# A ternary feed-forward layer whose down projection takes its activation as two halves in the short format

## The reference

```
def _tlin(x, w, s):
    return jnp.einsum('bsi,oi->bso', x, w) * s
h = jax.nn.silu(_tlin(x, w1_w, w1_s)) * _tlin(x, w2_w, w2_s)
h = jax.nn.gelu(_tlin(h, h1_w, h1_s), approximate=False)
h = jax.nn.gelu(_tlin(h, h2_w, h2_s), approximate=False)
return _tlin(h, w3_w, w3_s)
```

## Time and profile before

| | |
|---|---|
| median of 3 runs | 1860.53 us (1858.65 to 1861.09) |
| profiled execution, its own time | 1849.88 us |
| its span, first to last instruction | 1848.1 us |
| PE busy in the span | 1516.0 us (82%) |
| DVE busy | 1064.0 us (58%) |
| ACT busy | 729.2 us (39%) |
| mean granted clock of TensorE | 0.915 |

### The profile page before, as it was taken

How to read it: one execution, slowest core, us unless ns; L and a number is a source line. 1 busy time by engine, 2 the same in 40 slices (tenths; PEclk the granted TensorE clock), 3 DMA queues, 4 the chain that set the end, 5 groups by cost and what they waited for, 6 DMA issues and landing times.

```text
span 1848.1 us, 26160 instructions
## 1 busy us (share of the span) xinstructions
PE 1516.0 (82%) x8925; PEld 1098.1 (59%) x8925; DVE 1064.0 (58%) x2296; ACT 729.2 (39%) x1214; POOL 103.1 (6%) x129
## 2 busy tenths in 40 slices
PE   7999999777778967777788999999888888873455
PEld 5666666555534435556567787878484848463344
DVE  3434434877777648777883525261667777754222
ACT  2312221666635655445512222222274747561111
POOL 0000000000000000000000000000000000003111
PEclk9999999899989978889899999999989989985777
DMA  9330000300000000000094000001000000001553
GB/s 320 115 114 0 0 0 6 148 11 11 11 1 1 1 11 1 11 11 11 0 340 131 1 2 1 2 1 31 6 2 6 0 5 5 0 0 56 174 156 103
DMA packets 66241, 83.35 MB, mean 45 GB/s; under 512 B 13395, under 2 KB 61004, under 8 KB 65998
## 3 DMA queue, kind: packets, MB, share of 16 engines
q1 hardware_dynamic: 63774, 66.83, 11.9%
q10 hardware_dynamic: 512, 11.11, 1.8%
q0 software_dynamic: 1872, 4.27, 0.6%
HBM read 60.49 MB, written 33.10 MB: 51 GB/s over the span
## 4 chain that ended last, share of the span: by engine, by line
issue 40%; PE 34%; DVE 11%; DVEq 4%; ACT 4%; SPq 2%; DMA 2%; ACTq 1%; POOL 1%; POOLq 0%
PE bank L1756 6%; PE bank L1757 6%; DVE plo L820 3%; PE bank L1819 3%; PE bank L1576 3%; PE bank L1596 2%; PE bank L1578 2%; DMA jx<-copy_routed 2%; PE bank L1530 2%; PE bank L1688 1%; ACT hq L1323 1%; ACT phi L1264 1%; PE bank L1860 1%; ACTq L1322 1%; PE bank L1713 1%
## 5 line engine op out<-in xcount | busy, mean ns | idle before, releaser
L820 DVE TENSOR_TENSOR plo<-e,phi 120x512 f16<-120x512 f32 x256 | 185.5, 740 | 86.8 <-ACT phi L1264 81.0
L1596 PE MATMUL bank<-Q,Kpad 128*120 128x256 f16 x1024 | 209.9, 288 | 8.6 <-ACT MBT L1256 8.6
L1270 ACT ACTIVATE e<-bank 120x512 f32<-120x512 f32 x256 | 152.8, 597 | 68.3 <-PE bank L1601 38.7
L775 DVE TENSOR_REDUCE MB<-bank 128x4 bf16<-128x480 f32 x256 | 149.5, 647 | 17.6 <-PE bank L1578 12.1
L1264 ACT ACTIVATE phi<-e 120x512 f16<-120x512 f32 x256 | 158.1, 622 | 0.0
L1576 PE MATMUL bank<-Kpad,Q 128*128 128x480 f16 x256 | 107.7, 421 | 55.8 <-issue 32.0
L1600 PE MATMUL bank<-MBT,selm 128*120 128x256 bf16 x512 | 144.3, 282 | 0.0
L1601 PE MATMUL bank<-MBT,sels 128*120 128x256 bf16 x512 | 144.0, 281 | 0.0
L1619 PE MATMUL bank<-V,phi 120*128 120x34 f16 (+1 forms) x1024 | 85.4, 176 | 56.0 <-DVE plo L820 54.4
L1596 PEld LDWEIGHTS bank<-Q,Kpad 128*120 128x120 f16 x1024 | 117.3, 138 | 10.7 <-ACT MBT L1256 10.7
L1494 PE MATMUL bank<-xT,winT 128*127 128x512 f32 (+1 forms) x256 | 114.8, 594 | 4.7 <-ACTq L1183 4.7
(11 more groups left out here) (271 smaller groups left out, 2945.2 us busy)
## 6 DMA issues: line engine op xcount, KB each, us to landing
copy_routed<-zeros SPq DMA_DIRECT2D x1, 17028.0 KB, 65.6
jw<-in_w1e SPq DMA_DIRECT2D x23, 256.0 KB, 2.8
jw<-in_w2e SPq DMA_DIRECT2D x23, 256.0 KB, 3.0
h1w<-copy_h1T SPq DMA_DIRECT2D x1, 4096.0 KB, 17.8
h2w<-copy_h2T SPq DMA_DIRECT2D x1, 4096.0 KB, 14.2
ctxp<-in_ctxT SPq DMA_DIRECT2D x13, 240.0 KB, 2.6
jx<-copy_routed SPq DMA_DIRECT2D x23, 132.0 KB, 2.7
jb<-in_b2e SPq DMA_DIRECT2D x23, 128.0 KB, 3.4
```

What stands on the lines that cost most here:

```text
L775: dve.tensor_reduce(MB[:, t, h0 // 8, SK + h0 % 8:SK + h0 % 8 + 4], bank[2 + n % 4][:, 0:4 * SK].rearrange("p (h k) -> p h k", h=4), AX.X, ...
L820: dve.tensor_tensor(plo[:, u % 3, :], e32[:, u % 3, :], phi[:, u % 3, :], ALU.subtract).then_inc(s.lo, 1)
L1270: act.activation(e32[:, u % 3, :], bank[2 + u % 4][0:SK, :], ACT.Exp).then_inc(s.exp, 1)
L1596: pe.matmul(ps, Kpad[:, v, r, g, b * SK:b * SK + SK], Q2[:, g, qs], start=(v == 0), stop=False)
```

## The change

The down projection moves into `second`, and so into both of its copies. It takes the activation as the halves `hah` and `hal`, two passes for each tile of f3, in the short format in the first copy. ScalarE writes the second gelu into `raw` (semaphore `Ff.g2`), and VectorE splits it (`Ff.h2`), after the splits of the next pair's input. VectorE's check in the first pair takes in f3 too. f3 is now copied and loaded as the other matrices are.

```
-        for t, w in ((wq2, "wq2"), (wk2, "wk2"), (wv2, "wv2"), (wo2, "wo2"), (f3, "f3T")):
+        for t, w in ((wq2, "wq2"), (wk2, "wk2"), (wv2, "wv2"), (wo2, "wo2")):
...
+    w_in["f3T"] = nc.dram_tensor("copy_f3T", [HID, D], F32, kind="Internal").ap()
...
+                sp.dma_start(f3[:], kp(w_in["f3T"])).then_inc(ld_h1, 16)
...
                     for q in range(2):
                         low_bits(h2w[:, 4 * q:4 * q + 4, :], low2[:], lowmax[:, q, 0:1])
                         dve.drain()
+                    low_bits(f3[:].rearrange("p k n -> p (k n)"), low2[:, 0:HT * D], lowmax[:, 2, 0:1])
+                    dve.drain()
                     dve.tensor_tensor(lowall[:, 0:1], lowmax[:, 0, 0:1], lowmax[:, 1, 0:1], ALU.add)
+                    dve.drain()
+                    dve.tensor_tensor(lowall[:, 0:1], lowall[:, 0:1], lowmax[:, 2, 0:1], ALU.add)
                     dve.drain().then_inc(Ff.low, 1)
...
                 with dve.If(i < PAIRS - 1):
                     split_inputs(i + (4 * 5 + 2))
+                for t in range(HT):
+                    dve.drain()
+                    dve.wait_ge(Ff.g2, i * HT + (t + 1))
+                    split(hah[:, t, :], hal[t][:], raw[:, t % 2, :]).then_inc(Ff.h2, 1)
...
                     act.wait_ge(Ff.p2, i * HT + (t + 1))
-                    act.activation(ha[:, t, :], bank[[2, 3, 0, 1][t % 4]][:, :], ACT.Gelu,
-                                   scale=s12[:, 3, t:t + 1]).then_inc(Ff.h2, 1)
+                    if t < 2:
+                        act.wait_ge(Ff.h1, i * HT + (HT - 1 + t))
+                    else:
+                        act.wait_ge(Ff.h2, i * HT + (t - 1))
+                    act.activation(raw[:, t % 2, :], bank[[2, 3, 0, 1][t % 4]][:, :], ACT.Gelu,
+                                   scale=s12[:, 3, t:t + 1]).then_inc(Ff.g2, 1)
...
         def second(i, short):
             for t in range(HT):
                 if t >= 4:
-                    pe.wait_ge(Ff.h2, i * HT + (t - 3))
+                    pe.wait_ge(Ff.g2, i * HT + (t - 3))
...
                 last.then_inc(Ff.p2, 1)
+            for t in range(TT):
+                for k in range(HT):
+                    if t == 0:
+                        pe.wait_ge(Ff.h2, i * HT + (k + 1))
+                    ps = bank[4 + t // 2][:, (t % 2) * D:(t % 2) * D + D]
+                    for v, half in enumerate((hah[:, k, tok(t)], hal[k][:, tok(t)])):
+                        w = f3[:, k, :]
+                        if short:
+                            half, w = half.bitcast(F32R), w.bitcast(F32R)
+                        last = pe.matmul(ps, half, w, start=(k == 0 and v == 0), stop=(k == HT - 1 and v == 1))
+                if t % 2:
+                    last.then_inc(Ff.out, 1)
...
                 with pe.If(long2 != 0):
                     second(i, False)
-                for t in range(TT):
-                    for k in range(HT):
-                        if t == 0:
-                            pe.wait_ge(Ff.h2, i * HT + (k + 1))
-                        last = pe.matmul(bank[4 + t // 2][:, (t % 2) * D:(t % 2) * D + D], ha[:, k, tok(t)],
-                                         f3[:, k, :], start=(k == 0), stop=(k == HT - 1))
-                    if t % 2:
-                        last.then_inc(Ff.out, 1)
```

More of the change, by code:

```diff
@@ L319, in build @@
         sem("f_" + n) for n in ("gate", "silu", "h0", "p1", "h1", "p2", "h2", "out"))
-    Ff.xs, Ff.m0, Ff.g1, Ff.low, Ff.lowsum, Ff.long = (
-        sem("f_" + n) for n in ("xs", "m0", "g1", "low", "lowsum", "long"))
+    Ff.xs, Ff.m0, Ff.g1, Ff.g2, Ff.low, Ff.lowsum, Ff.long = (
+        sem("f_" + n) for n in ("xs", "m0", "g1", "g2", "low", "lowsum", "long"))
     Df = Signals()
@@ L365, in build @@
     LD_CONST, LD_L0, LD_IN, LD_OUT, LD_L1 = 8 * 16, 5 * 16, 2 * 16, 3 * 16, 7 * 16
-    LD_L2, LD_L3X, LD_L3 = (5 + 3 + 2 * 2 + 2) * 16, 4 * 16, 2 * 16
+    LD_L2, LD_L3X, LD_L3 = (4 + 3 + 2 * 2 + 2) * 16, 4 * 16, 2 * 16
     w_in = {w: nc.dram_tensor("copy_" + w, [m, HID], F32, kind="Internal").ap()
             for w, m in (("f1T", D), ("f2T", D), ("h1T", HID), ("h2T", HID))}
+    w_in["f3T"] = nc.dram_tensor("copy_f3T", [HID, D], F32, kind="Internal").ap()
     xbuf = nc.dram_tensor("copy_routed", [SLOTS, CELL], F32, kind="Internal").ap()
@@ L437, in _ @@
                 sp.dma_start(m32[:], a["mask"][0:TOK, :].rearrange("(t p) k -> p t k", p=128)).then_inc(mask_ready, 16)
-                sp.wait_ge(w_copied, 16 * 4)
+                sp.wait_ge(w_copied, 16 * 5)
                 sp.dma_start(f1, kp(w_in["f1T"])).then_inc(ld_h1, 16)
@@ L480, in _ @@
                             (ld_l1, LD_L1), (ld_l2, LD_L2), (mask_ready, (0, 16 * 5, 16 * 9)[sum(phases > q for q in (2, 4))]),
-                            (w_copied, 64), (ld_h1, 48 if phases > 2 else 0), (ld_h2, 16 if phases > 5 else 0),
+                            (w_copied, 80), (ld_h1, 64 if phases > 2 else 0), (ld_h2, 16 if phases > 5 else 0),
                             (ld_l3x, LD_L3X if phases > 6 else 0), (ld_l3, LD_L3 if phases > 6 else 0),
@@ L749, in attention @@
                 dve.wait_ge(ld_l2, LD_L2)
-                dve.wait_ge(ld_h1, 48)
+                dve.wait_ge(ld_h1, 64)
             first_mask = 16 * (5 if L is L2X else 1)
```

## The result

The change makes the kernel slower: 1872.46 us (median of 6 runs, 1869.95 to 1876.05) against 1860.81 us (6 runs, 1858.65 to 1863.72), a ratio of 1.0062 with a 95% interval of 1.0049 to 1.0076. The forecast was 1867 us and slower. The profiled execution took 1876.05 us with a span of 1874.0 us and a mean granted clock of 0.903.

What follows compares the result with a forecast made beforehand. TensorE was taken to bound layer 2's feed-forward stage. Three returns +7.6, last pair −5.1 and first pair +4.3 sum to +6.8 us; 1860.5 + 6.8 = 1867 us, range 1850 to 1876.

Steps and rivals of the forecast that it cites:

- The passes: Down projection on TensorE: 64 short passes of 256 columns replace 32 f32 matmuls, taken at 0.12 us a step.
- the rival of slow passes: Down-projection passes bound by their weight loads, 0.19 us instead of 0.12: +10.4 us, 1878 us; chance 0.05.
- The wait for the eighth half: Fifteenth down pass waits 0.95 us for tile 8's halves; with the shorter steps, 5.1 us won per pair.
- The jump: Jump over the float copy at a pair's end: takes 3.67 us, cover only 1.9 us.
- The return: Loop return right behind the jump, with an empty queue: 3.9 us, being 3.3 as now plus 0.6.
- The price of a return: Each of three loop returns costs 0.9 us of delay plus 1.6 us of slow clock, 2.5 us: +7.6.
- The clock: After 6 us of TensorE idling at each return, a granted 0.50 costs 1.6 us (bounds 0 and 2.4).
- The first pair: Check of f3's low bits on VectorE delays gelu and TensorE: 4.0 us, plus 0.3 for slow clock, +4.3.
- The last pair: No return; the jump over the float copy is covered by the next layer's wait for the residual: −5.1 us.
- Both jumps stay hidden: Rival: at pair ends, fetching goes on while passes run and brings the loop's end along: −15.5 us, 1845; chance 0.08.
- only the return is cheap: Rival: the loop return takes 0.2 us because its target is still held: −9.2 us, 1851; chance 0.08.
- the deeper queue: Rival: TensorE's queue holds 32 passes, 3.84 us of cover, hiding the first jump: +1.6 us, 1862; chance 0.04.

## Why the prediction was right, and where its sizes were off

*The passes*: right. The step is 0.12 us (49 steps from 1027.92 to 1033.86 make 0.121), and the rival of slow passes falls.

*The wait for the eighth half*: right in kind and nearly in size. The fifteenth pass starts 2.51 us after the first, forecast 2.62; the idle time in the row is 0.70 us, since a pass is recorded until its last result.

*The jump*: right. It starts 2.0 us before the last pass and took 3.31 to 3.83 us, forecast 3.67. *The return*: the term was too small, 4.6 us (median) where 3.9 was taken. The 0.6 us that the forecast added for the packet behind the jump's own was meant for exactly this and should have been 1.3: that packet does come first, and the return's own takes 1.8 to 2.2 us beside it. A return alone takes 3.4 to 3.8 us in the kernel with the down projection between the two.

*The price of a return*: 2.5 us forecast. The stretch from the first down pass to the next gate pass grew from 13.63 (1017.23 to 1030.86) to 14.86 us in the first pair, +1.2 instead of +0.9, and by 1.2 and 1.7 in the next two: +4.1. The 64 gate passes behind the return took 17.1 to 17.2 us before and 19.2, 18.5 and 18.7 after: +5.1, or 1.7 for a slow spell, where 1.6 was forecast. Together +9.2 instead of +7.6.

*The clock*: right in kind. A granted 0.50 follows the holes of 6 us. With the down projection between the branches the holes are 1.49, 1.83 and 1.93 us, and only the middle one has slow passes behind it (a granted 0.58 in the 3.1 us from 1120.9; 1.00 behind the other two).

*The first pair*: +3.9 for the wait, forecast 4.0. The 0.3 for a longer slow spell was not there: the passes behind the wait are slow from the first one on, before and after, and were so for 3.3 us before and 2.8 after. The window shows 4.8 = 3.9 + 1.2 − 0.3.

*The last pair*: the step that failed. "The jump is covered: −5.1." The gain was there: from the first down pass to layer 3's first matmul it is 10.46 us where it was 15.75, −5.3 (−3.6 in the window, which holds 1.6 of a slow spell), and the jump was over before the wait for the residual. But the forecast asked only whether the jump itself was covered and not what the code behind it brings. Before, 32 matmuls stood between the jump and layer 3, and the next block arrived under them. Now layer 3's code follows at once, and after three of its matmuls the second hole of 2.12 us opens, with a slow spell behind it: +4.0. I read it as the next block of code coming late, since nothing else holds these matmuls and one packet of code arrives between 1318.9 and 1320.6. It starts at 1319.05, lands at 1320.40, and the matmul follows 1.45 us later; behind the own packets of the jumps at the pairs' ends the jump is over 1.3 to 1.5 us after the landing. The hole is in all four profiles in which layer 3's code has this place behind a fetching jump, 1.4 to 1.5 us after a landing each time. The padded kernels bear this out: with 64 matmuls of padding the hole is there (1.90 us), and with 32, where layer 3's code stands 32 matmuls earlier in its block, it is not:

```profile
1319.88 3.48 PE L1544 MATMUL bank<-ctxp,wk 128*128 128x240 f32 x16 [1.80 <-DVEq L1054]
```

The sum: +9.2 + 3.6 − 5.3 + 4.0 = +11.5 for the forecast's +7.6 + 4.3 − 5.1 = +6.8. Of the 4.7 us between the two sums 4.0 are a hole that wasn't forecast and 1.6 returns sized too low; the first and the last pair give back 0.9. So the mechanism of the returns was right, and the time fell inside the range because the range was wide enough for a term that the forecast did not have.

*The rivals.* "Both jumps stay hidden" and "only the return is cheap" fall by the 6 us holes and 4.6 us returns; the deeper queue falls by the 16 passes in hand at the jump, 2.0 us of cover. The rule of a queue of 64 entries (the Trainium skill, TensorE: Matmul & The Clock Gate) does not hold for what stands in hand at a branch. The rule on taken branches held in part: a target that isn't held is fetched, but the store's whole capacity decides, not a window of two pages. And the forecast read it by the count of rows in the body, 706 and 819; the padding shows that not even the count of instructions decides, but that of the blocks touched. The figure of 1845 us for hidden jumps turned out to be near the time of the kernels whose loop is held (1840.0 to 1844.7 us), though there no fetch is hidden: none takes place.

## What to carry to other kernels

Before code is put into or moved out of a branch on an engine's main loop, read the branch lines: a duration of 3 us instead of 0.2 says that the loop's code is fetched anew in each round, and then what counts is how many passes stand between one taken branch and the next. Cheaper passes shorten that cover too. If an unlikely copy must stay, choose between two whole loops once instead of jumping over the copy in every round: that turned this change, together with a check made earlier, from 1.0062 into 0.9908. It won nothing (1.0014) where the fetches had been covered. And ask of code behind a jump when its second block will come.

## What was unexpected of the hardware

- 32 f32 matmuls of padding that never run cost 1.2% of the time (0.9923 to 1.0046), and twice as many in another place nothing (0.9922). The step is all or nothing: nine code packets in a pair, or none.
- Two fetches back to back slow each other: 4.5 to 5.1 us for a return behind a jump, 3.3 to 3.9 for either alone. The jump over the gates' copy in the first pair takes 6.35 to 6.41 us in every kernel: its packet starts 3.8 us after it instead of 1.0, while the DMA engines are over 90% busy; that the load is the reason isn't shown.
- Removing three covered fetches in each later pair of the kernel before brought nothing measurable (1.0014, 1.0 to 1.0027).
